# A GNN and mixture-of-experts layer: the edge attributes' split moved from GpSimd to ScalarE and VectorE, and VectorE's order rewritten

## The reference

```python
def mish(x):
    return x * jnp.tanh(jax.nn.softplus(x))
src, dst = (edge_index[0], edge_index[1])
edge_feat = jnp.concatenate([x[src], x[dst], edge_attr], axis=-1)
h = mish(edge_feat @ W1 + b1)
messages = mish(h @ W2 + b2)
agg = jax.ops.segment_sum(messages, dst, num_segments=x.shape[0])
```

## Time and profile before

| | us |
|---|---|
| median of 3 runs | 1414.67 |
| lowest and highest | 1414.13, 1416.09 |
| profiled execution | 1416.24 |
| its span (first to last instruction) | 1414.6 |
| PE busy | 1145.5 (81%) |
| DVE busy | 1108.9 (78%) |
| POOL busy | 913.7 (65%) |
| ACT busy | 852.9 (60%) |

### The profile page before, as it was taken

The page is one execution under the profiler, slowest core; times in us unless marked ns, Lnnn a source line. Parts: engine busy times, 40 slices in busy tenths (PEclk is TensorE's granted clock), DMA queues, the critical chain, the costliest instruction groups (busy, mean ns, idle before and its releaser), DMA issues. The chain is left out here.

```text
span 1414.6 us, 20672 instructions
## 1 busy us (share of the span) xinstructions
PE 1145.5 (81%) x5823; PEld 912.1 (64%) x5824; DVE 1108.9 (78%) x1627; ACT 852.9 (60%) x1061; POOL 913.7 (65%) x755
## 2 busy tenths in 40 slices
PE   0992888889889899899898889889838997559972
PEld 0671666777677677677677777767626775558861
DVE  3840579999999999999999999999864876743364
ACT  1311667777777777777777777777843543333341
POOL 1333788898888888889889889888431210454410
PEclk9996899999999999999999999999968997679965
DMA  5534554554554554455455455455210111634452
GB/s 145 200 116 98 117 107 96 109 114 96 107 111 101 102 111 106 98 111 110 98 109 112 96 110 113 96 106 108 81 38 23 37 44 44 189 106 131 127 164 101
DMA packets 113398, 148.00 MB, mean 105 GB/s; under 512 B 55389, under 2 KB 63980, under 8 KB 113225
## 3 DMA queue, kind: packets, MB, share of 16 engines
q0 software_dynamic: 40912, 101.69, 32.8%
q1 hardware_dynamic: 72377, 45.20, 11.6%
q10 hardware_dynamic: 16, 0.02, 0.0%
HBM read 136.29 MB, written 15.66 MB: 107 GB/s over the span
## 5 line engine op out<-in xcount | busy, mean ns | idle before, releaser
L696 POOL DMA_INDIRECT gath<-dst_table,idx_sl x166 | 283.8, 1709 | 49.7 <-issue 27.2
L828 PE MATMUL ps<-W2l,hTh 128*128 128x512 f32 x664 | 264.2, 398 | 0.0
L828 PE MATMUL ps<-W2h,hTh 128*128 128x512 f32 x664 | 263.5, 397 | 0.0
L721 POOL TENSOR_TENSOR msg_lo<-act,msg_hi 128x1024 fp32r<-128x1024 f32 x83 | 213.3, 2570 | 33.9 <-DVE msg_hi L800 33.9
L706 POOL DMA_INDIRECT gath<-src_table,idx_sl x166 | 171.6, 1034 | 76.7 <-issue 50.3
L806 DVE TENSOR_TENSOR dloc<-idx_sl,block_off 128x2 f32<-128x2 int32 x83 | 180.3, 2172 | 14.9 <-DMA idx_sl<-idx_scr 14.9
L828 PE MATMUL ps<-W2h,hTl 128*128 128x512 f32 x664 | 174.9, 405 | 0.4 <-DVE hTl L795 0.2
L828 PEld LDWEIGHTS ps<-W2l,hTh 128*128 128x128 f32 x664 | 125.7, 189 | 30.6
L828 PEld LDWEIGHTS ps<-W2h,hTh 128*128 128x128 f32 x664 | 126.0, 190 | 26.4
L793 DVE TENSOR_TENSOR agg<-agg,ps 125x512 f32 x166 | 112.9, 680 | 31.0 <-DVE agg L793 23.3
L746 ACT ACTIVATE act<-act 128x1024 f32<-128x1024 f32 x83 | 88.2, 1062 | 77.6 <-DVE act L782 77.6
(11 more groups left out here) (315 smaller groups left out, 2852.2 us busy)
## 6 DMA issues: line engine op xcount, KB each, us to landing
f_w_raw<-in_L_ffn_w_dram SPq DMA_DIRECT2D x32, 512.0 KB, 4.6
ea_sl<-ea_scr SPq DMA_DIRECT2D x166, 32.0 KB
ea_scr<-in_edge_attr_dram POOLq DMA_DIRECT2D x1, 5000.0 KB, 20.6
w_raw<-in_L_gnn_W_dram SPq DMA_DIRECT2D x3, 1024.0 KB, 18.6
idx_sl<-idx_scr SPq DMA_DIRECT2D x166, 1.5 KB, 1.7
gath<-src_table,idx_sl POOLq DMA_INDIRECT x166, 4.2
gath<-dst_table,idx_sl POOLq DMA_INDIRECT x166, 5.2
x_raw<-in_x_dram SPq DMA_DIRECT2D x5, 500.0 KB
```

Of the source, the lines that this page charges most:

```text
L696: pool.indirect_dma_start(out=gath[:, k, j, :], out_offset=None, in_=dst_table[:, :], in_offset=bass.IndirectOffsetOnAxis(ap=idx_sl[:, b % ...
L721: nc.gpsimd.tensor_tensor(msg_lo[:, m % 2], act2[:, m % 3], f32(msg_hi[:, m % 2]), ALU.subtract).then_inc(S["msg_lo_ready"], 1)
L828: return nc.tensor.matmul(ps_2[:, r % 2, j, :], part[:, r % 2, d, j * P:(j + 1) * P], weights[:, d, :], start=False, stop=last)
```

## The change

- SP loads each tile's edge attributes twice, into the left and the right half of a wider `ea_sl`; `ea_hl` is gone. PE transposes `ea_sl` itself, so that the transpose holds the attributes twice, in its upper and its lower 64 partitions. ACT's copy rounds both; DVE then subtracts the lower half's rounded copy from the transpose, in a new instruction (`eaT_lo`).
- POOL's copy and subtraction (L713, L715) are gone, and `msg_lo` is moved from the end of POOL's step to its start.
- On DVE the two `agg` additions go behind `hTl` and `msg_hi`, and `dloc` and `onehot` to the end of the step, behind L818.
- On ACT the second Ln goes ahead of the copy to `eaT`.
- On PE the low-part matmuls of lin2's first tile go ahead of the transposes of the edge attributes, the second tile's stay behind. The gathers' transposes run in the order 2, 3, 0, 1; those of parts 0 and 1 wait for `eaT_lo`. The transposes wait for one `summed` fewer.

The diff, cut to its core:

```diff
@@ sync @@
-                        sp.wait_ge(S["split"], q - IN + 1)
+                        sp.wait_ge(S["eaT_ps"], q - IN + 1)
...
-                        sp.dma_start(ea_sl[:, k, j, :], ea_scr[bass.ds(first, P), :]).then_inc(ea_in[k], 16)
+                        for half in range(2):
+                            sp.dma_start(ea_sl[:, k, j, half * EDIM:(half + 1) * EDIM], ea_scr[bass.ds(first, P), :]).then_inc(ea_in[k], 16)
@@ gpsimd: this at the step's start, ahead of the gathers; it stood at the end @@
+                m = s - 3
+                if exists(m):
+                    pool.wait_ge(S["msg_hi_ready"], m + 1)
...
-                    nc.gpsimd.tensor_copy(ea_hl[:, k, :, 0:EDIM], ea_sl[:, b % IN]).then_inc(S["ea_hi"], 1)
-                    pool.wait_ge(S["ea_hi"], b + 1)
-                    nc.gpsimd.tensor_tensor(ea_hl[:, k, :, EDIM:2 * EDIM], ea_sl[:, b % IN], f32(ea_hl[:, k, :, 0:EDIM]), ALU.subtract).then_inc(S["split"], 1)
@@ scalar @@
+                if second:
+                    act.wait_ge(S["sq2"], g + 1)
+                    nc.scalar.activation(a2, a2, ACT.Ln, bias=half_col[:], scale=0.5).then_inc(S["ln2"], 1)
                 if exists(n):
                     act.wait_ge(S["eaT_ps"], n + 1)
@@ vector @@
+                t = s + 1
+                if exists(t):
+                    dve.wait_ge(S["eaT_hi"], t + 1)
+                    nc.vector.tensor_tensor(eaT[EDIM:, t % 2, :], ps_1[EDIM:, t % 2, 0, :], f32(eaT[EDIM:, t % 2, :]), ALU.subtract).then_inc(S["eaT_lo"], 1)
...
+                if exists(m):
+                    dve.wait_ge(S["dst_ready"], m + 1)
+                    nc.vector.tensor_tensor(onehot[:, m % 2], iota_n[:].unsqueeze(1).to_broadcast([P, 2, NE]),
+                                            dloc[:, 2 * m:2 * m + 2].unsqueeze(2).to_broadcast([P, 2, NE]), ALU.is_equal).then_inc(S["onehot_ready"], 1)
@@ tensor @@
+                if exists(r):
+                    pe.wait_ge(S["h_lo"], r + 1)
+                    lo_tile(0)
                 if exists(n):
                     k = n % 2
-                    pe.wait_ge(S["split"], n + 1)
+                    pe.wait_ge(*loaded(ea_in, IN, n, 64))
...
-                        pe.wait_ge(S["summed"], (n - 4) * 2)
+                        pe.wait_ge(S["summed"], (n - 5) * 2 + 1)
...
+                    lo_tile(1).then_inc(S["lin2_ps"], 1)
...
-                    pe.wait_ge(S["eaT_ready"], n + 1)
                     pe.wait_ge(*loaded(both_gath, GA, n, 32))
-                    for d in range(KC):
+                    if n >= 5:
+                        pe.wait_ge(S["summed"], (n - 4) * 2)
+                    for d in (2, 3, 0, 1):
+                        if d == 0:
+                            pe.wait_ge(S["eaT_lo"], n + 1)
```

More of the change, by code:

```diff
@@ L627, in edge_phase @@
         idx_sl = sb("idx_sl", [P, IN, 2, 3], I32)
-        ea_sl = sb("ea_sl", [P, IN, 2, EDIM])
-        ea_hl = sb("ea_hl", [P, 2, 2, 2 * EDIM], F32R)
+        ea_sl = sb("ea_sl", [P, IN, 2, 2 * EDIM])
         eaT = sb("eaT", [2 * EDIM, 2, E2], F32R)
@@ L648, in edge_phase @@
         src_gath, both_gath = slots("src_gath", GA), slots("both_gath", GA)
-        names = ("ea_hi split dst_ready eaT_ps eaT_ready gath_read lin1_ps exp1 inc1 sq1 ln1 quot1 h_ready h_hi h_lo lin2_ps "
+        names = ("dst_ready eaT_ps eaT_hi eaT_lo gath_read lin1_ps exp1 inc1 sq1 ln1 quot1 h_ready h_hi h_lo lin2_ps "
                  "exp2 inc2 sq2 ln2 quot2 msg_ready msg_hi_ready msg_lo_ready onehot_ready sum_ps summed w3_in w3_hi w3_lo").split()
@@ L690, in _ @@
             for s in range(FIRST, LAST + 1):
+                m = s - 3
+                if exists(m):
+                    pool.wait_ge(S["msg_hi_ready"], m + 1)
+                    if m >= 2:
+                        pool.wait_ge(S["sum_ps"], m - 1)
+                    nc.gpsimd.tensor_tensor(msg_lo[:, m % 2], act2[:, m % 3], f32(msg_hi[:, m % 2]), ALU.subtract).then_inc(S["msg_lo_ready"], 1)
                 b = s + 2
@@ L756, in _ @@
                         act.wait_ge(S["lin1_ps"], n - 1)
[L757 to L760, removed]
+                    nc.scalar.activation(eaT[:, n % 2, :], ps_1[:, n % 2, 0, :], ACT.Copy).then_inc(S["eaT_hi"], 1)
                 if first:
@@ L785, in _ @@
                     nc.vector.tensor_scalar(act2[:, g % 3], act2[:, g % 3], EXP_MAX, 1.0, ALU.min, ALU.add).then_inc(S["inc2"], 1)
+                if exists(r):
+                    nc.vector.tensor_tensor(hTl[:, r % 2], act1[:, r % 2], f32(hTh[:, r % 2]), ALU.subtract).then_inc(S["h_lo"], 1)
+                if exists(m):
+                    if m >= 2:
+                        dve.wait_ge(S["sum_ps"], m - 1)
+                    dve.wait_ge(S["msg_ready"], m + 1)
+                    nc.vector.tensor_copy(msg_hi[:, m % 2], act2[:, m % 3]).then_inc(S["msg_hi_ready"], 1)
                 if exists(a):
@@ L819, in _ @@
                                                    op0=ALU.subtract, op1=ALU.mult).then_inc(S["msg_ready"], 1)
+                if exists(n):
+                    dve.wait_ge(*loaded(idx_in, IN, n, 32))
+                    nc.vector.tensor_tensor(dloc[:, 2 * n:2 * n + 2], idx_sl[:, n % IN, :, 2], block_off[:, 2 * n:2 * n + 2], ALU.subtract).then_inc(S["dst_ready"], 1)
+                if exists(m):
+                    dve.wait_ge(S["dst_ready"], m + 1)
+                    nc.vector.tensor_tensor(onehot[:, m % 2], iota_n[:].unsqueeze(1).to_broadcast([P, 2, NE]),
+                                            dloc[:, 2 * m:2 * m + 2].unsqueeze(2).to_broadcast([P, 2, NE]), ALU.is_equal).then_inc(S["onehot_ready"], 1)
                 lo_parts(s)
@@ L850, in _, with lo_tile @@
                     hi_tile(1)
+                def lo_tile(j):
+                    for d in range(KC):
+                        ins = lin2(j, d, hTl, W2h, d == KC - 1)
+                    return ins
+                if exists(r):
+                    pe.wait_ge(S["h_lo"], r + 1)
+                    lo_tile(0)
                 if exists(n):
                     k = n % 2
-                    pe.wait_ge(S["split"], n + 1)
+                    pe.wait_ge(*loaded(ea_in, IN, n, 64))
                     if n >= 2:
@@ L856, in _ @@
                     if n >= 5:
-                        pe.wait_ge(S["summed"], (n - 4) * 2)
+                        pe.wait_ge(S["summed"], (n - 5) * 2 + 1)
                     for j in range(2):
-                        ins = nc.tensor.transpose(ps_1[:, k, 0, j * P:(j + 1) * P], f32(ea_hl[:, k, j, :]), ident[:])
+                        ins = nc.tensor.transpose(ps_1[:, k, 0, j * P:(j + 1) * P], ea_sl[:, n % IN, j, :], ident[:])
                     ins.then_inc(S["eaT_ps"], 1)
                 if exists(r):
-                    pe.wait_ge(S["h_lo"], r + 1)
-                    for j in range(2):
-                        for d in range(KC):
-                            ins = lin2(j, d, hTl, W2h, d == KC - 1)
-                    ins.then_inc(S["lin2_ps"], 1)
+                    lo_tile(1).then_inc(S["lin2_ps"], 1)
                 if exists(n):
                     k = n % 2
-                    pe.wait_ge(S["eaT_ready"], n + 1)
                     pe.wait_ge(*loaded(both_gath, GA, n, 32))
-                    for d in range(KC):
+                    if n >= 5:
[3 more added lines that the diff above has]
+                            pe.wait_ge(S["eaT_lo"], n + 1)
                         for j in range(2):
```

## The result

The changed kernel takes 1567.41 us (median of 4 runs, 1566.9 to 1570.71), the kernel before 1414.4 us on the same chip (1414.07 to 1416.09). The ratio is 1.108, with a 95% interval of 1.107 to 1.110: 10.8% slower. The profiled execution took 1566.9 us, its span is 1565.3.

What follows compares the result with a forecast made beforehand. Bound: a PE-ACT-DVE circle, 10.37 + 0.42 + 0.93 + 0.93 - 1.04 = 11.61 us, plus 1.04 for the clock, 12.65 a step; 79 steps give +156.7, less 9, +147.7: 1562 us, range 1470 to 1600.

Steps and rivals of the forecast that it cites:

- The step: Time from one pair's lin2 to the next in the edge phase: from 10.667 us to 12.65, over 79 steps.
- The circle: Chain from `onehot` through PE, ACT and DVE back to `onehot`, said to set 11.61 us a step at full clock.
- two large new terms: On PE, the sum's four matmuls and four low-part matmuls ahead of the transposes: each adds 0.93 us a step.
- `onehot`'s tail: End of DVE's step: `dloc` and `onehot` behind L818 add 0.42 us together; the run forecasts gave `onehot` 0.33.
- The second Ln: On ACT, done before the transposes land, so it leaves the chain of waits: 1.04 us less a step.
- the hidden circle: Chain through PE, ACT and DVE in the kernel before: 10.37 us, only 0.3 us shorter than the step.
- the lock: DVE's `dloc` stands still behind POOL's `msg_lo` for about 2.2 us of each step in the kernel before.
- The clock: PE's 2.48 us pause lowers its clock: 1.56 us in two steps of three, 1.04 us a step.
- the first rival: The clock stays up on PE: step 11.61 us, +63.5 us, 1478 us in all; chance 20%.
- Start and end: Ends of the edge phase: -5.9 us between pairs 2 and 3, -3 at the very start, -9 together.
- POOL itself has no room: POOL's queue in the kernel before: gathers, split and `msg_lo` fill 10.58 us of a step.
- The rival on the other side: Transposes' results arrive before ACT wants them; DVE's and ACT's own circle sets 9.71 us, 1328 us; chance 4%.

Runs made afterwards that it cites:

- x3: Changed kernel with six throwaway 512-column matmuls more per step in PE's pause before the wait for `onehot`: 1482 us, step 11.603 us.
- x2: Changed kernel with the edge attributes' transposes back ahead of all low-part matmuls on PE, `onehot` still last: 1411 us, step 10.728 us.
- x1: Changed kernel with only `onehot` moved back to an early place on DVE, between `hTl` and `msg_hi`: 1373 us, step 10.256 us.
- x4: Kernel before the change with only `dloc` moved behind L818, to the end of DVE's step: 1394 us, step 10.409 us.
- x5: Changed kernel with both `onehot` early on DVE and the transposes ahead of all low-part matmuls on PE: 1332 us, step 9.701 us.
- x9: Changed kernel with `onehot` and transposes early, and src gathers issued one step further ahead (four gather buffers, five index slots): 1325 us, step 9.619 us.
- x7: Kernel before the change with only `onehot` moved behind L818, to the end of DVE's step: 1583 us, step 12.799 us.
- x8: Changed kernel with `onehot` and transposes early, ACT's Exp ahead of the `eaT` copy and second Ln, `msg_hi` and `onehot` earlier still: 1357 us.

## Why the prediction was right

It named 1562 us; measured were 1567.

- **The step.** Predicted 12.65 us, measured 12.696: 3.6 us of the 5.
- **The circle.** 11.61 us by adding rows of the kernel before; 11.63 with the clock held up (x3). Its two large new terms were 0.93 us each. The low-part matmuls measured 0.88 (x2). `onehot`'s tail and the sum's matmuls were 0.93 + 0.33; x1, which takes away both, is 11.60 - 10.26 = 1.34 shorter. The second Ln was not moved by itself in any run, but both sums, 10.26 and 11.61, meet what was measured only with its 1.04 taken off. And the hidden circle of the kernel before, 10.37 us, which no wait showed as the bound, came to light at 10.41 when the lock was taken away (x4). The waits came as forecast: PE 2.31 us for `onehot`, and ACT for the transposes 1.9 us in x3, where the clock is up (forecast 1.8), 3.43 in the slowed step shown.
- **The clock.** I took 1.56 us for a drop and two steps in three, 1.04. Measured were 1.09 on the mean; the longest step is 1.53 above 11.63. It is not that two steps in three lose 1.56 and the third nothing: from the first high-part matmul to the transposes it is 5.12 us at full clock (x3), and longer than that in 57 of 78 steps of the changed kernel, by up to 1.57; the rest is lost in the sum's matmuls, and even the shortest step in mid-phase has 11.93. The share was a guess between two bounds, and it lay well by luck: the row of 2.01 us bore out that the clock would drop, not how often. My pause of 2.48 us counted from the last matmul's issue, and in that measure it is 608.21 - 605.74 = 2.47; the profile's 2.31 counts from its end, as does the 2.01 with which I compared it, so the margin between the two was smaller than I took it to be.
- **The rule against it.** The Trainium skill's advice (in "TensorE: Matmul & The Clock Gate", section "Why this matters for your kernels") to allow no idle gaps over about 3 us would have given the first rival, 1478 us (the prediction calls it the second there, by mistake). x3 shows that time, 1482, for a kernel whose marked pauses of PE in the phase are at most 0.81 us. With the pause of 2.31 the trace disagrees with the rule: the clock was 0.90.
- **Start and end.** Predicted -9, measured -9.6, but put together otherwise. From pair 2 to pair 3 it is 175.81 - 164.10 = 11.71 us instead of 17.48, as I had said. Of the 3 us that I gave to the transposes not waiting for GpSimd's split, 1.05 were there at pair 2 (164.10 against 165.15) and none at pair 0, which starts at 144.57, before at 144.2. The drain gave 2.8, which I had not looked at, so that the sum came out right by luck. (The rivals' sums use -11 where the forecast uses -9; the prediction gives no reason, and it is 2 us.)
- **What failed.** "POOL itself has no room" took 10.58 us of occupied time for fixed work. In x4 a step takes 10.4 us with the same work of GpSimd. It had no weight for the changed kernel, where POOL idles 4.6 us before `msg_lo` in a long step, but made me expect too little of x4.
- **The sign.** The rival on the other side, 1328 us, asked that `onehot` be free of L818. In x1, where it is, the time is 1373; x5 and x9, which have the transposes early as well, take 1332 and 1325. That this is near 1328 does not show that rival's circle.

## What to carry to other kernels

An instruction that nothing waits for long in the profile may be the one that two engines' circle goes through: before moving work to the end of an engine's step, ask which other engine's first instruction needs it, and add up the way back to it. A wait that ends last hides the circle that would end next; compute that circle's length from the trace before paying for the wait's removal, for it caps the gain. And a pause of TensorE on such a circle can cost more than itself, since what comes behind it may run at the lower clock; giving the engine throwaway matmuls in the pause measures that share.

## What the runs showed of the hardware

- A pause of 2.31 us in each step of about 12.7 (the changed kernel) went with a granted clock of 0.90 and a mean step longer by 1.09 us; one of 2.38 in x7 with 0.90 too. Pauses of 1.38 to 1.55 us in each step of 10.7 (x2) left it at 1.00, and so did pauses of about 0.77 us with the rest filled (x3).
- Throwaway matmuls (six of 512 columns a step) made the changed kernel 85 us faster (x3).
- Instructions of GpSimd and VectorE that lie beside one another can take longer: `dloc` 0.15 to 2.36 us, the cast of `hTh` 0.69 to 1.37 (x8), GpSimd's split 0.83 (x4, the step shown) and 1.45. Their busy time is therefore not a measure of their work.
